# One P.V group of 36 key tiles per pair of images, and the convolution split between ScalarE and GpSimd

## The reference

```python
q = x @ Wq + bq;  k = (x @ Wk + bk) * scaling;  v = x @ Wv + bv
lepe = lax.conv_general_dilated(v, dw_w, ..., feature_group_count=C) + dw_b   # 5x5, depthwise
attn = jnp.einsum('bhnd,bhmd->bhnm', qr, kr) + mask
out = jnp.einsum('bhnm,bhmd->bhnd', jax.nn.softmax(attn, axis=-1), vr)
out = out + lepe
return out @ Wo + bo
```

## Time and profile before

| | us |
|---|---|
| median of 3 runs (3563.69 to 3568.47) | 3567.22 |
| the profiled execution, its own time | 3568.93 |
| its span, first to last instruction | 3567.1 |
| DVE busy in it (73%) | 2620.2 |
| ACT busy (57%) | 2029.5 |
| POOL busy (46%) | 1648.6 |
| PE busy (96%) | 3426.9 |

### The profile page before, as it was taken

One profiled execution on the slowest core, in us unless ns is written; L12 is line 12 of the kernel. 1 busy time (PEld: TensorE's weight loads), 2 busy tenths in 40 slices (PEclk: granted clock), 3 DMA queues, 4 the chain that ended last, 5 costly groups with the idle time before them and its releaser, 6 DMA issues. The chain is left out here.

```text
span 3567.1 us, 96354 instructions
## 1 busy us (share of the span) xinstructions
PE 3426.9 (96%) x30684; PEld 2651.6 (74%) x30684; DVE 2620.2 (73%) x6494; ACT 2029.5 (57%) x3660; POOL 1648.6 (46%) x862
## 2 busy tenths in 40 slices
PE   8699999999999999999999999999699999999988
PEld 5377777777777777777777777777487777878867
DVE  8588888888888888888888888888565564644457
ACT  4366666666666666666666666666344454455533
POOL 5555655565565665555566556556400100005112
PEclk9799999999999999999999999999799999999989
DMA  7542242233224224223322422221520110000011
GB/s 265 185 130 95 68 136 92 84 98 115 95 73 131 92 80 124 92 95 93 111 92 80 124 92 95 74 95 64 157 85 15 43 58 16 28 1 1 1 42 43
DMA packets 111820, 308.48 MB, mean 86 GB/s; under 512 B 11592, under 2 KB 72955, under 8 KB 91163
## 3 DMA queue, kind: packets, MB, share of 16 engines
q1 hardware_dynamic: 110629, 306.27, 27.4%
q10 hardware_dynamic: 1054, 0.48, 0.0%
HBM read 252.38 MB, written 54.31 MB: 86 GB/s over the span
## 5 line engine op out<-in xcount | busy, mean ns | idle before, releaser
L782 DVE CUSTOM_DVE_ANT_0 c_S<-c_Sps,mask_tiles 128x768 f32<-128x768 f32 x1728 | 1619.6, 956 | 420.1 <-PE c_Sps L835 367.1
L723 ACT ACTIVATE c_PT<-c_Tps 128x512 f32<-128x512 f32 x2592 | 1428.7, 605 | 871.9 <-PE c_Tps L846 809.2
L691 POOL TENSOR_SCALAR c_S<-c_S,c_row_max 128x2304 f32<-128x2304 f32 x576 | 1411.1, 2450 | 950.5 <-DVE c_row_max L793 950.5
L846 PE MATMUL c_Tps<-ident,c_S 128*128 128x128 f32 x10368 | 1398.8, 272 | 4.1 <-ACT c_PT L723 4.1
L846 PEld LDWEIGHTS c_Tps<-ident,c_S 128*128 128x128 f32 x10368 | 1225.5, 140 | 151.2 <-ACT c_PT L723 9.7
L835 PE MATMUL c_Sps<-c_K,c_Q 96*128 (+1 forms) x3456 | 853.5, 328 | 41.8 <-DVEq L763 22.6
L859 PE MATMUL c_Ops<-c_PT,c_V 128*32 128x256 f32 x10368 | 619.2, 382 | 0.8 <-ACT c_PT L723 0.8
L859 PEld LDWEIGHTS c_Ops<-c_PT,c_V 128*32 128x32 f32 x10368 | 307.4, 109 | 243.7 <-issue 48.4
L835 PEld LDWEIGHTS c_Sps<-c_K,c_Q 96*128 96x128 bf16 x3456 | 314.8, 98 | 201.1 <-issue 145.1
L1385 DVE TENSOR_SCALAR_CACHE_REDUCE l_S<-l_Sps 128x384 f32<-128x384 f32 x432 | 240.3, 558 | 294.7 <-PE l_Sps L1208 268.3
L1121 ACT ACTIVATE ln2T<-l_Tps 128x384 f32<-128x384 f32 x432 | 196.5, 491 | 404.9 <-PE l_Tps L1229 404.9
(11 more groups left out here) (204 smaller groups left out, 1677.5 us busy)
## 6 DMA issues: line engine op xcount, KB each, us to landing
mask_tiles<-in_mask SPq DMA_DIRECT2D x144, 1152.0 KB, 7.6
numerators<-c_O SPq DMA_DIRECT2D x288, 64.0 KB
mask_tiles<-numerators SPq DMA_DIRECT2D x7, 2304.0 KB, 8.6
q_parts<-f_parts SPq DMA_DIRECT2D x12, 576.0 KB, 4.9
k_parts<-f_parts SPq DMA_DIRECT2D x12, 576.0 KB
...
```

The lines of the kernel that those rows point to most:

```text
L691: pool.tensor_scalar(S[:, slot, :], S[:, slot, :], -1.0, row_max[:, slot:slot + 1], ALU.mult, ALU.add).then_inc(shifted, 1)
L723: act.activation(dst, src, ACT.Exp, scale=-1.0).then_inc(exp_done, 1)
L782: dve.tensor_tensor_reduce(out=S[:, r % ROW_SLOTS, cols(CH, c)].rearrange("p (k n) -> p k n", k=2), in0=Sps[:, n % S_SLOTS, :, 0:GW], in1= ...
L846: last = pe.transpose(Tps[:, g % T_SLOTS, cols(P, k)], S[:, (2 * b + t) % ROW_SLOTS, cols(P, kt)], ident[:, :])
```

## The change

Four things are done. P.V of two images becomes one group of 36, after T1 and a1 of the next even image; odd images have none. PT gets a second place for the first 8 key tiles of an even image (`pt_place`, `EARLY = 8`), so that ACT waits for `pt_used` at its third group instead of its first. The taps leave DVE: ACT writes the product of window and tap into one buffer, `product`, after its exponentials (image 0, group 1), (image 1, group 6) and (image 2, group 1); POOL adds it to `conv` after the shifts of rows 4, 6 and 7. A product waits for `conv_step`, that is until the sum before it has read the buffer; a sum waits for `product_ready`. The rest (counts, constants, the store's wait) follows from these.

The core of the diff:

```diff
-            def values(ip, half, group):
...
-                for i in V_TILES[group]:
+            def values(ip, half):
+
+                pe.wait_ge(o_taken, 2 * ip + half + 1)
+                pe.wait_ge(v_placed, 2 * (ip // HEAD_PAIRS) + half + 1)
+                pe.wait_ge(exp_done, TG * (B * ip + 2 * half + 2) + T_SLOTS)
+                for i in range(2 * TILES):
...
                     if b % 2 == 0:
-                        behind(1)
                         ahead(1)
+                        behind()
+                        ahead(2)
                         transposes(ip, b, 2)
                         transposes(ip, b, 3)
-                        ahead(2)
                         transposes(ip, b, 4)
                         ahead(3)
...
-                        values(ip, b // 2, 0)
+                        transposes(ip, b, 5)
                         ahead(3)
...
+        product = sb("product", [P, N // 2])
+        PRODUCT_AFTER = ((0, 1), (1, 6), (2, 1))
+        SUM_AFTER = (4, 6, 7)
...
+        def pt_place(half, image, kt):
+
+            if image:
+                return EARLY + TILES + kt
+            return half * EARLY + kt if kt < EARLY else EARLY + kt
...
+                            if row in SUM_AFTER:
+                                tap = qp * PER_PAIR + SUM_AFTER.index(row)
+                                pool.wait_ge(conv_step, CONV_STEPS * h + tap + 2)
+                                alone(pool)
+                                pool.wait_ge(product_ready, TAP_SLOTS * h + tap + 1)
+                                alone(pool)
+                                pool.tensor_tensor(conv[:, hp, :], conv[:, hp, :], product[:, :], ALU.add).then_inc(conv_step, 1)
...
+            def conv_product(ip, k):
+                h = ip // HEAD_PAIRS
+                tap = (ip % HEAD_PAIRS) * PER_PAIR + k
+                if k == 0:
+                    act.wait_ge(vpad_in, 16 * (h + 1))
+                    alone(act)
+                act.wait_ge(conv_step, CONV_STEPS * h + tap + 2)
+                alone(act)
+                window = vpad[:, bass.ds((h % 2) * HALF_IN + tap // 5 * WP + tap % 5, HALF_OUT)].rearrange("p (h w) -> p h w", w=WP)
+                act.activation(product[:, :].rearrange("p (h w) -> p h w", w=W), window[:, :, 0:W], ACT.Copy,
+                               scale=taps[:, bass.ds(tap, 1)]).then_inc(product_ready, 1)
...
-                    if b % 2 == 0 and g in (0, 3):
-                        act.wait_ge(pt_used, V_GROUPS * (B // 2 * ip + b // 2) + 1 + g // 3)
-                    if b % 2 and g == 0:
-                        act.wait_ge(pt_used, V_GROUPS * (B // 2 * ip + b // 2 + 1))
+                    if b % 2 == 0 and g == EARLY // 4:
+                        act.wait_ge(pt_used, B // 2 * ip + b // 2 + 1)
...
                     act.activation(dst, src, ACT.Exp, scale=-1.0).then_inc(exp_done, 1)
+                    if (b, g) in PRODUCT_AFTER:
+                        conv_product(ip, PRODUCT_AFTER.index((b, g)))
...
-                dve.scalar_tensor_tensor(out=dst, in0=window[:, :, 0:W], scalar=taps[:, bass.ds(tap, 1)],
-                                         in1=dst, op0=ALU.mult, op1=ALU.add).then_inc(conv_step, 1)
...
-                        if (r, c) in TAP_AFTER:
-                            conv_tap(ip, TAP_AFTER.index((r, c)))
```

More of the change, by code:

```diff
@@ L529, in layer0_core @@
         sb, ps = buffers(nc, ctx, "c")
+        EARLY = 8
         sem = sem_maker(nc, ctx, "c")
@@ L679, in _ @@
             pool.memset(taps[:, TAPS:TAP_SLOTS], 0.0).then_inc(taps_padded, 1)
-            ROUNDS = HEAD_PAIRS * ROWS // ROW_SLOTS
+            pool.sem_inc(conv_step, 1)
             with pool.Fori(0, HEADS // 2) as hh:
                 for hp in range(2):
-                    pool.wait_ge(conv_stored, 16 * (2 * hh + hp + 1))
+                    h = 2 * hh + hp
+                    pool.wait_ge(conv_stored, 16 * (h + 1))
                     alone(pool)
                     pool.memset(conv[:, hp, :], 0.0).then_inc(conv_step, 1)
-                    with pool.Fori(0, ROUNDS) as i:
-                        for slot in range(ROW_SLOTS):
-                            pool.wait_ge(max_ready, ROW_SLOTS * ((2 * hh + hp) * ROUNDS + i) + slot + 1)
+                    with pool.Fori(0, HEAD_PAIRS) as qp:
+                        for row in range(ROWS):
+                            slot = row % ROW_SLOTS
+                            pool.wait_ge(max_ready, ROWS * (h * HEAD_PAIRS + qp) + row + 1)
                             alone(pool)
@@ L720, in exp @@
                         t, first = group[0]
-                        dst = PT[:, b % 2, first:first + 4, cols(P, t)]
+                        place = pt_place(b // 2, b % 2, first)
+                        dst = PT[:, place:place + 4, cols(P, t)]
                         src = Tps[:, g % T_SLOTS, :].rearrange("p (k q) -> p k q", q=P)
                     act.activation(dst, src, ACT.Exp, scale=-1.0).then_inc(exp_done, 1)
+                    if (b, g) in PRODUCT_AFTER:
+                        conv_product(ip, PRODUCT_AFTER.index((b, g)))
             def take_o(ip, p, half):
-                act.wait_ge(pt_used, V_GROUPS * (B // 2 * ip + half + 1 + 1))
+                act.wait_ge(pt_used, B // 2 * ip + half + 1 + 1)
                 if half == 0:
@@ L847, in transposes @@
                 last.then_inc(t_ready, 1)
-            def values(ip, half, group):
-                if group == 0:
-                    pe.wait_ge(o_taken, 2 * ip + half + 1)
-                    pe.wait_ge(v_placed, 2 * (ip // HEAD_PAIRS) + half + 1)
-                pe.wait_ge(exp_done, TG * (B * ip + 2 * half + (2 if group else 1)) + T_SLOTS)
-                for i in V_TILES[group]:
+            def values(ip, half):
[3 more added lines that the diff above has]
+                for i in range(2 * TILES):
                     j = i % COLS
@@ L858, in values @@
                     b = 2 * half + image
-                    last = pe.matmul(Ops[32 * j:32 * (j + 1), image, :], V[:, b * TILES + kt, :], PT[:, image, kt, :],
+                    last = pe.matmul(Ops[32 * j:32 * (j + 1), image, :], V[:, b * TILES + kt, :], PT[:, pt_place(half, image, kt), :],
                                      start=kt < COLS, stop=kt >= TILES - COLS)
@@ L871, in ahead, with behind @@
                             scores(ip + 1, 1 - p, r - ROWS, c)
-                    def behind(group):
+                    def behind():
                         if b:
-                            values(ip, b // 2 - 1, group)
+                            values(ip, b // 2 - 1)
                         elif not start:
-                            values(ip - 1, 1, group)
+                            values(ip - 1, 1)
                     transposes(ip, b, 0)
@@ L882, in pair @@
                     if b % 2 == 0:
-                        behind(1)
                         ahead(1)
+                        behind()
+                        ahead(2)
                         transposes(ip, b, 2)
                         transposes(ip, b, 3)
-                        ahead(2)
                         transposes(ip, b, 4)
                         ahead(3)
+                        transposes(ip, b, 5)
+                        transposes(ip, b, 6)
+                        ahead(4)
+                        transposes(ip, b, 7)
+                        ahead(5)
+                        transposes(ip, b, 8)
                     else:
@@ L895, in pair @@
                         ahead(2)
-                        values(ip, b // 2, 0)
+                        transposes(ip, b, 5)
                         ahead(3)
-                    transposes(ip, b, 5)
-                    transposes(ip, b, 6)
-                    ahead(4)
-                    transposes(ip, b, 7)
-                    ahead(5)
-                    transposes(ip, b, 8)
+                        transposes(ip, b, 6)
+                        transposes(ip, b, 7)
+                        ahead(4)
+                        transposes(ip, b, 8)
+                        ahead(5)
             for r in range(LEAD):
@@ L914, in _ @@
             pair(PAIRS - 1, 1, end=True)
-            for group in range(1, V_GROUPS):
-                values(PAIRS - 1, 1, group)
+            values(PAIRS - 1, 1)
 def layer1_attention(nc, a, s, ident, conv_bias, x1, ln2, ln2T, sums, first_num, first_in, first_den, den_in):
```

28 lines of the change are left out of this document (9 added, 19 removed).

## The result

The changed kernel takes 3798.5 us (median, 3797.0 to 3799.4); the kernel before took 3566.4 in the same comparison (3563.7 to 3568.5). The ratio is 1.0646, 95% interval 1.0634 to 1.0659: slower by 232 us. I had forecast 3700 and a range of 3620 to 3752. The sign and the handshake's wait came out, the size did not: the clock fell, and PE's own order gained less than forecast.

What follows compares the result with a forecast made beforehand. PE's own order was taken to set the pace. A pair: 31.90 + 2.4 + 0.25 = 34.55 us for 32.72; 72 pairs +132, borders +7, giving 3706, taken as 3700 for overlap; range 3620 to 3752.

Steps and rivals of the forecast that it cites:

- the handshake's wait: PE ahead of T1 of image 2: waits through POOL's sum and ACT's product, 2.4 us a pair; chance 0.82.
- ScalarE's own wait: ACT before the product: idle until POOL's sum releases it, some 1.8 us in 72 instances.
- The second wait: PE ahead of T0 of the next pair: waits for row 0's shift behind the third sum, 0.24 us.
- The borders: At seven borders of heads the memset of `conv`, 1.06 us, is no longer hidden: 7 us in all.
- The duration of the sum: POOL's add of 1152 elements: 2.32 us, drawn from adds of 384 and 768 elements.
- The bound of 2.48: Upper limit for POOL's add: one and a half times the row of 768 elements.
- my line: POOL's add: straight line through 0.995 us for 384 and 1.656 for 768 elements, giving 2.32 for 1152.
- What PE gains: PE's order with merged P.V, nobody making it wait: 31.90 us a pair, 0.82 less, 59 us over 72.
- The clock: P.V behind PE's pause: rival that it runs at half rate, +4.3 us a pair, some 4010; chance 0.04.
- the overlap: Neighbouring ACT and POOL instructions: some 0.1 us a pair, 7 us in all, lowering 3706 to 3700.
- "nothing": End of the stage: larger P.V adds 1.3 us, about as much comes back elsewhere, so no net change.
- PE's gain alone: Rival at ACT's product: buffer already free, no wait, PE keeps 0.82 us a pair, 3509; chance 0.10.
- A cheap add: Rival: POOL's add and ACT's product at lower bounds (1.10, 0.84), 3568 to 3576, no change; chance 0.04.

Runs made afterwards that it cites:

- e6: Changed kernel with two float32 product buffers (EARLY = 4), products moved and sums put where GpSimd is idle; 3557.1 us, ratio 0.9964 to the kernel before.
- e8: Changed kernel with 5 matmuls of 256 float32 columns, results unused, filling TensorE's pause ahead of T1 of image 2; 3737.7 us, ratio 1.0476 to the kernel before.
- e12: Changed kernel with its single product buffer in bf16 instead of float32; 3748.5 us, ratio 1.0507 to the kernel before.
- e5: Changed kernel's TensorE order, convolution back on VectorE with its taps moved beside P.V; 3562.5 us, ratio 0.9983 to the kernel before.
- e10: e6 with the chunks of scores spread differently in images 1 and 3; 3541.4 us, ratio 0.9926 to the kernel before.
- e3: Changed kernel with 20 unused transposes filling TensorE's pause ahead of T1 of image 2; 3839.6 us, ratio 1.0753 to the kernel before.
- e7: Changed kernel with every add over 576 of its 1152 elements only; 3636.6 us, ratio 1.0194 to the kernel before.
- e2: Kernel before's TensorE order and P.V groups of 12 and 24, with the changed kernel's split convolution and single buffer; 3775.9 us, ratio 1.0581.
- e1: Changed kernel's TensorE order and PT, with the convolution back on VectorE at its old taps; 3653.8 us, ratio 1.0244 to the kernel before.

## Why the forecast failed, point by point

**The handshake's wait: right.** Forecast 2.42 ahead of T1 of image 2. Measured on the intervals, 18.63 less the 16.19 of e6 is 2.44. This is partly luck in the links. From a0 of image 1 (1497.80), the sum ended at 6.74 for 6.46, ScalarE started 0.44 behind it and not 0.17 (together 7.18 for 6.63), the product ended at 8.44 for 7.82. From the product's end to T1 it then took 0.53 for my 0.77, 0.10 of it because the exponential started before the product's end: T1 started at 8.97 for 8.6. PE itself would have been there at 6.40, not 6.18, since VectorE held up the chunk ahead. PE's weight loads were thus 2.57 late against where it would have been, of which the following chunks, then no longer held up, gave 0.13 back. ScalarE's own wait ahead of the product was 2.34 for 1.8; the product beside P.V waits too, for 3.4, and costs nothing, as foretold.

**The second wait: right.** 0.24 forecast, 16.34 less 16.19 = 0.15 measured, released by `c_S` of GpSimd. **The borders: wrong, by some 10 us.** I had added 7 us for the memset of `conv`. But the kernel before has its own price at each of the seven borders, 0.43 and 0.55 in the two pairs beside it, 7 us in all; at full clock (e8) one pair is longer by 0.56, 4 us in all. The change adds nothing there and saves some 3.

**The duration of the sum: undersized.** 2.32 forecast, 2.64 measured. The line went through a row whose second operand, `f_parts`, is bf16, and an all-float32 row. e12 shows what that is worth: 2.39 for 1152 elements with a bf16 operand. With three float32 sizes (0.995 for 384, 1.417 for 576, 2.642 for 1152) the line is 0.19 + 2.13 ns per element. The bound of 2.48 was too low as well. By the Trainium skill, "GPSIMD Engine Reference", 3.1 Elementwise, the estimate had been 2.53; it was nearer than my line, and the trace's mixed types were why. My remark that both sizes of the trace lie below the rate of the Trainium skill's section was wrong for the smaller: 0.995 us for 384 is 2.59 ns per element, and its 4497 ns for 2048 are 2.20.

**What PE gains: wrong, 0.34 for 0.82 a pair.** The failed sentence is "it does not bind, though around the end of an image its chunks are as dense as PE's". VectorE's mean load (22.9 of 32 us) says nothing of three chunks in a row. The rows of 1.00 and 0.88 are in e6 and e5; e10 removes one in each half pair, and gains 16 us. Against the forecast's 31.90 this is 0.48 a pair, 35 us. The trace of before held its price, passes 0.89 apart where VectorE has no idle time, and 1.08 where a row maximum lies between:

```profile
1511.71 0.95 DVE L782 CUSTOM_DVE_ANT_0 c_S<-c_Sps,mask_tiles 128x768 f32<-128x768 f32 x1
...
1512.59 0.15 DVE L793 TENSOR_REDUCE c_row_max<-c_part_max 128x1 f32<-128x3 f32 x1
1512.79 0.96 DVE L782 CUSTOM_DVE_ANT_0 c_S<-c_Sps,mask_tiles 128x768 f32<-128x768 f32 x1
...
1513.68 0.95 DVE L782 CUSTOM_DVE_ANT_0 c_S<-c_Sps,mask_tiles 128x768 f32<-128x768 f32 x1
```

**The clock: wrong, chance 0.04 for what happened.** The mechanism was in the rivals, with a price of 4.3 us in every pair. What happened is between "no" and that: about every second pair, mostly 1.7 us each (5.78 for 4.09), since the clock comes back within the P.V. It is 61 us. e8 shows them by filling the pause, with T1 where it was, and e3 has none of these slow groups either. I had held against it that the waits of other engines had never stopped PE so long in this stage: that was no evidence, since the change was what would first do it. What the runs show of pauses: with PE idle for 2.33 ahead of T1 (matmuls, the changed kernel) 38 of 72 pairs have a slow P.V, with 2.08 (e12) 23, with 1.1 (e7) none. The two of e2, 0.96 and 1.66 in a pair, bring none, nor do its seven of 2.2. Length alone doesn't decide it: of the changed kernel's 56 pauses of 2.32 to 2.37, 31 have a slow P.V behind them and 25 have not.

**The sum again.** Forecast 31.90 + 2.4 + 0.25 = 34.55 a pair. Measured 31.90 + 0.48 + 2.44 + 0.15 + 0.85 = 35.82. The difference, 1.27 in 72 pairs, is 91 us; 3706 + 91 = 3797, for 3798.5 measured. The steps that failed are then the clock, which the sum put at nothing, by 61 us, and the sum's first term, PE's own period, by 35. The two waits of GpSimd and ScalarE are off by less than 7 us in all; the overlap for which I took 6 us off is inside the 2.44.

**Luck in that total.** The border's 7 us are in the 3706 and were not there, and something else filled their place. From the start of the last P.V to the end the kernel before takes 1044.5 us and the changed one 1053.1, where I had said "nothing". e1 and e5, with the taps on VectorE, take 1044.1 and 1044.2 there, and all runs with the convolution on ScalarE and GpSimd 1048.5 to 1053.2. Most of it arises in steps inside the second layer, which is not touched; no run takes it apart. So the profiled execution's 228.8 us are 223 of 72 pairs (3.10 each), 3 less at the borders and 8.5 more behind the stage. The 8.5 also hide a part of every gain: e6 is 15.5 us ahead of the kernel before at its last P.V, and 7.6 at its end.

**Of the rivals.** "PE's gain alone" (3509) would have been wrong even without a wait: e5 and e6 have none of it and take 3557 to 3563. "A cheap add" was excluded by the add itself.

What stays open: why the clock falls in about every second pair and not in each, though the pauses are alike. Then the gaps of PE in e3, which came with a longer loop, and the 8 us behind the last P.V. I took neither apart.
